# Graph network kernel: five TensorE signals by drains, one GpSimd wait per slot instead of three

## Chip, cores and metric

One core of one Trainium2 chip runs the kernel. The metric is the device time of one execution in microseconds (us), median over the runs. Lower is better. A core has five engines that run their own instruction streams and meet only at semaphores: TensorE (PE, matmuls), VectorE (DVE), ScalarE (ACT), GpSimd (POOL) and SyncE (SP, which issues plain DMAs). Data of the kernel is float32 throughout.

## What is computed

A layer norm with ReLU on 12500 nodes of 128 features, then one graph layer over 200000 edges whose destinations are sorted, and a residual. Cut to what matters:

```python
h = relu(layernorm(x))                                   # 12500 x 128
l1 = linear(h)                                           # per node
w = silu(silu(rbf(dist) @ fc_w1) @ fc_w2) @ fc_w3        # 200000 x 128, per edge
g = l1[edge_src]                                         # gather of 200000 rows
msg = [w00*gs*sh0, w11*dot(gv, sh1), w01*gs*sh1, w10*gv*sh0]   # 200000 x 256
agg = segment_sum(msg, edge_dst) / count
x = x + sc(h) + tanh(agg_s @ alpha_w) * linear2(agg)
```

## The kernel before, in words

**Three stages.** The first stage (some 65 us) normalises the nodes and stores `l1` as `lin_table` in HBM. The second stage, which takes nearly all the time, walks over the edges. The third stage (some 12 us) finishes the last node blocks.

**The walk over the edges.** Edges are cut into 261 groups of 768 (`GROUP`, six tiles of 128). Four groups make a step (`SLOTS` = 4, `u` is the slot, `i` the step), and 65 steps and one short group make up the edges. Every engine has a function `body` with its own fixed order of work for slots `u` = 0 to 3; nothing but semaphores ties the engines together. Counters are compared with `n = i * SLOTS + u`, the group's number.

**GpSimd** (`gather`, L954) only gathers: for each group it issues six indirect DMAs of 128 rows from `lin_table` into the slot's six tiles of `lin_g` (L970, 1563 in all). There are four slots, so group n overwrites what group n-4 used. Before tile 0 it waits until `near_ready` shows group n-4 (L958), before tile 2 until `h2_done` reaches n (L964), before tile 4 until `sums_ready` shows group n-4 (L967). All three are counted up by TensorE. Each wait stands on a `nop`.

**TensorE** in iteration u does, in this order: `layer1` of group n+3 (L999, 4 matmul records), `layer2` of n+2 (L1008), `layer3` of n+1 (L1018, writes `ps_w`), `segment_sum` of n-1 (L1040, writes `ps_sums`), `near_layer` of n (L1030, 12 records, writes `ps_near`). The last matmul of each step carries the signal: `h1_done`, `h2_done`, `w_ready`, `sums_ready`, `near_ready`. `segment_sum` waits for ScalarE's copy of `ps_near` and for VectorE's `agg_ready`; `near_layer` waits for `msg_ready` of its group.

**ScalarE** in iteration u: `silu1` (L1139, after `h1_done`), `silu2` (L1145, after `h2_done`), `copy_w` of n+1 (L1167, after `w_ready`; the trace calls its output `key_all`), `scale_lin` of n+2 (L1157, six tiles, after the gather of n+2), `copy_near` of n (L1172, after `near_ready`).

**VectorE** in iteration u: `accumulate` of n-2 (L1474, two additions into `agg`, after `sums_ready`, with a register load from SBUF at L1469 ahead), `products` of n+2 (L1383 waits for the gather of n+2), `columns`, then `late` of n+1 (L1415 waits for `copy_w`; its last instruction L1423 signals `msg_ready`), and once in four groups the radial basis (L1333 to L1367). `late` of group n is the last reader of that group's slot of `lin_g`.

Of the kernel before, what the change touches and what calls it, by code (L numbers as in the profile page):

```python
# [37 lines left out]
P = 128  # L38
# [8 lines left out]
SLOTS = 4  # L47
# [4 lines left out]
SEG = QUAD // SEGS  # L52
UNIT = 2 * SEG
# [7 lines left out]
NEAR = P // HALVES  # L61
# [10 lines left out]
MSG = 8 * MUL  # L72
# [50 lines left out]
def gnn_kernel(nc, x, src, dst, sh, dist, node_vec, sc_ws, sc_wv, lin1_ws, lin1_wv,  # L123
# [44 lines left out]
    with ExitStack() as top:  # L168
        def sb(name, shape, dt=F32, ctx=top):
            return ctx.enter_context(nc.sbuf_tensor(name, shape, dt))  # L170
# [4 lines left out]
        w1 = sb("w1", [P, SEGS // 2, P])  # L175
        w2 = sb("w2", [P, P])
        w3 = sb("w3", [P, 2, P])
# [26 lines left out]
        with ExitStack() as st:  # L204
# [3 lines left out]
            def sem(name):  # L208
                return st.enter_context(nc.semaphore(name))
# [424 lines left out]
        with ExitStack() as st:  # L634
            def s2(name, shape, dt=F32):
                return sb(name, shape, dt, st)
# [21 lines left out]
            near_sums = s2("near_sums", [P, 2, MSG + 1])  # L658
            far_hot = s2("far_hot", [P, SLOTS, P])
# [7 lines left out]
            rbf = s2("rbf", [P, SEG])  # L667
            h1 = s2("h1", [P, 2, UNIT])
            h2 = s2("h2", [P, 2, UNIT])
            onehot = s2("onehot", [P, SLOTS, TILES, NEAR])  # L670
# [4 lines left out]
            msg = s2("msg", [P, 2, TILES, MSG + 1])  # L675
# [10 lines left out]
            ps_h1 = st.enter_context(nc.psum_tensor("ps_h1", [P, 512], F32))  # L686
            ps_h2 = st.enter_context(nc.psum_tensor("ps_h2", [P, 512], F32))
            ps_w = st.enter_context(nc.psum_tensor("ps_w", [P, 8 * P], F32))
            ps_near = st.enter_context(nc.psum_tensor("ps_near", [P, 512], F32))
# [9 lines left out]
            def sums_bank(i):  # L699

                return ps_h1 if last_group(i) else ps_sums

            def ps_nodes(i):
                return sums_bank(i)[:, 0:COLS]
# [19 lines left out]
            h1_done, h1_ready, h2_done, h2_ready = sem("h1_done"), sem("h1_ready"), sem("h2_done"), sem("h2_ready")  # L724
            w_ready, w_copied, w_read = sem("w_ready"), sem("w_copied"), sem("w_read")
            msg_ready, sums_ready = sem("msg_ready"), sem("sums_ready")
# [4 lines left out]
            near_ready, near_copied = sem("near_ready"), sem("near_copied")  # L731
# [9 lines left out]
            def held(i):  # L741

                return slice(0, TILES, HALVES) if isinstance(i, int) and i == ITERS else slice(0, TILES)
# [19 lines left out]
            def src_loads(s):  # L763

                return 16 * (s.full + (1 if s.phase else 0))
# [54 lines left out]
            with nc.Fori(0, passes):  # L820
                nc.sync.sem_clear(range(sems[0].num, sems[0].num + len(sems)))
                nc.all_engine_barrier()
                with nc.Block() as block:
# [128 lines left out]
                    @block.gpsimd  # L952
                    def _(pool):
                        def gather(s, u, first=False):  # L954
                            if not first:
                                if u == 0:
                                    pool.wait_ge(src_in[s.phase], src_loads(s))
                                pool.wait_ge(near_ready, s.i * SLOTS + u - SLOTS + 1)  # L958
                                pool.nop(nofuse=True)
                            rows = slice(0, LAST_ROWS if isinstance(s.i, int) and s.i == ITERS else P)  # L960
                            tiles = range(TILES)[held(s.i)]
                            for k, t in enumerate(tiles):
                                if not first and k == 2:
                                    pool.wait_ge(h2_done, s.i * SLOTS + u)  # L964
                                    pool.nop(nofuse=True)
                                if not first and k == 4:
                                    pool.wait_ge(sums_ready, s.i * SLOTS + u - SLOTS + 1)  # L967
                                    pool.nop(nofuse=True)
                                col = t % HALVES * PAIRS + t // HALVES
                                pool.indirect_dma_start(  # L970
                                    slot_tiles(s, u)[rows, t, :], None, lin_table,
                                    bass.IndirectOffsetOnAxis(ap=src_ix[rows, s.phase, u, col:col + 1], axis=0)).then_inc(gathered[u], 16)

                        for b in range(OB):
                            pool.wait_ge(lin_stored[b], 16 * (len(range(b, STEPS, OB)) + (REST if b == STEPS % OB else 0)))
                        for u in range(SLOTS):
                            gather(turn_of(0), u, first=True)
                        with pool.Fori(0, (ITERS - 2) // RING) as t:
                            for k in range(RING):
                                for u in range(SLOTS):  # L980
                                    gather(turn_in(t, 1, k), u)
                        for u in range(SLOTS):
                            gather(turn_of(ITERS - 1), u)
                        gather(turn_of(ITERS), 0)

                        for u in range(SLOTS):
                            pool.wait_ge(gathered[u], landed(turn_of(ITERS if u == 0 else ITERS - 1), u))
                        pool.dma_reset()

                    @block.tensor  # L990
                    def _(pe):
                        def layer1(i, k):
                            i, k = i + k // UNITS, k % UNITS
                            if k == 0:
                                pe.wait_ge(rbf_ready, i + 1)
                            at_least(pe, h1_ready, i * UNITS + k)
                            rows = slice(k * 4 * RBF, (k + 1) * 4 * RBF)
                            for part in range(2):
                                mm = pe.matmul(ps_h1[:, part * SEG:(part + 1) * SEG], w1[rows, 2 * k + part, :], rbf[rows, :],  # L999
                                               start=True, stop=True)  # L1000
                            mm.then_inc(h1_done, 1)

                        def layer2(i, k, first=False):
                            i, k = i + k // UNITS, k % UNITS
                            if first:
                                pe.wait_ge(h1_ready, k + 1)
                            at_least(pe, h2_ready, i * UNITS + k)
                            pe.matmul(ps_h2[:, 0:UNIT], w2[:], h1[:, k % 2, :], start=True, stop=True).then_inc(h2_done, 1)  # L1008

                        def layer3(i, u):  # L1010

                            i, u = i + u // SLOTS, u % SLOTS
                            if isinstance(i, int) and (i == ITERS or (i == 0 and u == 0)):
                                pe.wait_ge(h2_ready, i * UNITS + u + 1)
                            at_least(pe, w_copied, i * SLOTS + u)
                            cols = h2[:, u % 2, :].rearrange("p (c j) -> p j c", j=PAIRS)
                            for j in range(PAIRS):
                                mm = pe.matmul(ps_w[:, 2 * j * P:(2 * j + 2) * P], cols[:, j, :], w3[:], start=True, stop=True)  # L1018
                            mm.then_inc(w_ready, 1)

                        def near_layer(i, u):

                            n = i * SLOTS + u
                            pe.wait_ge(msg_ready, n + 1)
                            if isinstance(i, int) and i == ITERS:
                                pe.wait_ge(near_copied, n)
                            for j in range(PAIRS):
                                for half in range(1 if isinstance(i, int) and i == ITERS else HALVES):
                                    t = j * HALVES + half
                                    mm = pe.matmul(ps_near[half * NEAR:(half + 1) * NEAR, 0:MSG + 1], onehot[:, u, t, :], msg[:, u % 2, t, :],  # L1030
                                                   start=(j == 0), stop=(j == PAIRS - 1))
                            mm.then_inc(near_ready, 1)

                        def segment_sum(i, u):

                            n = i * SLOTS + u
                            pe.wait_ge(near_copied, n + 1)
                            if not last_group(i):
                                pe.wait_ge(agg_ready, n + 1)
                            pe.matmul(ps_nodes(i), far_hot[:, u, :], near_sums[:, u % 2, :], start=True, stop=True).then_inc(sums_ready, 1)  # L1040

                        def turn_early(n, k):

# [641 lines left out]
```

## Time and profile before

| | |
|---|---|
| median of 3 runs | 2211.73 us (2203.23 to 2214.47) |
| span of the profiled execution | 2483.8 us |
| of it, stage with the gathers | 68 to 2455 us |
| mean granted TensorE clock | 0.826 |
| DMA, mean | 63 GB/s |

The profiled execution took 272 us more than the median of the runs. The page gives per engine the busy time and its share of the span. Views of the trace give, for a line of the kernel, how often it ran, how long one took, and how long its engine stood idle ahead of it and what ended that idle time. "issue" there means that the profile shows nothing that was waited for, "remote" that a semaphore came whose sender the profile could not tell.

### The profile page before, as it was taken

The page shows a single profiled execution, that of the slowest core. Times are in us where ns is not written, and L with a number is a line of the kernel's source. Part 1 is how long each engine was busy: PE and PEld are TensorE (multiplying, and loading weights), DVE is VectorE, ACT ScalarE, POOL GpSimd, SP SyncE. Part 2 cuts the span into 40 slices and gives each one's busy share as a digit, 9 for nine tenths or more (in the row PEclk, how much of TensorE's full clock was granted, in tenths as well). Part 3 has the DMA queues.
Part 4 walks back from the last instruction along what each step waited for, and adds up shares of the span by engine and source line. Part 5 has one row for each costly group of instructions (what it writes and reads, how often), then busy time and mean ns, then how long its engine had stood idle before and what let it go on. Part 6 is the DMA issues. An engine that isn't in the chain of part 4 may idle for free. (4 is left out here: it accounts for less than half of the span.)

```text
span 2483.8 us, 34021 instructions
## 1 busy us (share of the span) xinstructions
PE 1811.4 (73%) x7969; PEld 1174.2 (47%) x7969; DVE 1783.0 (72%) x4669; ACT 1199.1 (48%) x3310; POOL 1578.4 (64%) x1624
## 2 busy tenths in 40 slices
PE   6577777787777777767677767667787776877777
PEld 6344444454444444444444434444554444544544
DVE  8577767767776777767676667767677776777777
ACT  6354545455454555444444344445444444445443
POOL 7566666666666666666666666666666666666563
PEclk9588878878888887788787878888888888888889
DMA  7322222222222222222122222222222222222222
GB/s 214 70 64 67 56 64 66 66 56 66 66 59 62 67 65 56 55 48 50 46 50 48 48 48 49 54 50 64 57 67 62 59 65 66 53 64 61 59 66 55
DMA packets 347699, 155.73 MB, mean 63 GB/s; under 512 B 237983, under 2 KB 322048, under 8 KB 347584
## 3 DMA queue, kind: packets, MB, share of 16 engines
q0 software_dynamic: 50016, 102.51, 15.7%
q1 hardware_dynamic: 296938, 51.75, 11.4%
q14 instruction: 86, 0.70, 0.1%
q8 instruction: 29, 0.48, 0.1%
q10 hardware_dynamic: 630, 0.29, 0.0%
HBM read 134.27 MB, written 20.15 MB: 62 GB/s over the span
## 5 line engine op out<-in xcount | busy, mean ns | idle before, releaser
L970 POOL DMA_INDIRECT lin_g<-lin_table,src_ix x1563 | 1530.0, 979 | 865.1 <-issue 441.5
L1157 ACT ACTIVATE lin_sh<-lin_g,harm 128x128 f32<-128x128 f32 x1563 | 483.8, 396 | 94.6 <-DMA lin_g<-lin_table,src_ix 87.6
L1040 PE MATMUL ps_sums<-near_sums,far_hot 128*128 128x257 f32 x520 | 208.0, 488 | 440.8 <-DVE agg L1474 206.0
L1030 PE MATMUL ps_near<-msg,onehot 128*64 128x257 f32 x3126 | 507.5, 471 | 1.2 <-DVE msg L1423 1.2
L1018 PE MATMUL ps_w<-w,h 128*128 128x256 f32 x1566 | 462.6, 440 | 28.2 <-ACT key_all L1167 18.5
L1018 PEld LDWEIGHTS ps_w<-w,h 128*128 128x128 f32 x1566 | 395.3, 272 | 135.4 <-issue 44.9
L999 PE MATMUL ps_h<-rbf,w 32*128 32x192 f32 x1044 | 277.0, 390 | 138.0 <-issue 67.1
L1415 DVE TENSOR_TENSOR msg<-lin_sh,key_all 128x576 f32<-128x576 f32 (+1 forms) x261 | 197.3, 756 | 249.9 <-ACT key_all L1167 209.5
L1167 ACT ACTIVATE key_all<-ps_w 128x768 f32<-128x768 f32 x261 | 213.5, 818 | 305.2 <-remote 188.6
L1030 PEld LDWEIGHTS ps_near<-msg,onehot 128*64 128x64 f32 x3126 | 241.3, 164 | 230.6 <-issue 175.7
L1383 DVE TENSOR_TENSOR lin_sh<-lin_g,ps_meta 128x576 f32<-128x576 f32 (+1 forms) x261 | 196.6, 753 | 212.2 <-DMA lin_g<-lin_table,src_ix 207.0
L1040 PEld LDWEIGHTS ps_sums<-near_sums,far_hot 128*128 128x128 f32 x520 | 105.1, 230 | 503.9 <-issue 387.7
L1172 ACT ACTIVATE near_sums<-ps_near 128x257 f32<-128x257 f32 x261 | 99.4, 381 | 474.1 <-remote 342.1
L999 PEld LDWEIGHTS ps_h<-rbf,w 32*128 32x128 f32 x1044 | 189.1, 212 | 228.0 <-issue 176.2
L1008 PE MATMUL ps_h<-h,w 128*128 128x384 f32 x522 | 278.8, 620 | 0.4 <-issue 0.3
L1474 DVE SCALAR_TENSOR_TENSOR agg<-ps_sums,at_lo,agg 128x257 f32 x260 | 126.1, 485 | 190.7 <-issue 188.0
L1401 DVE TENSOR_REDUCE dot<-lin_sh 128x192 f32<-128x576 f32 (+1 forms) x261 | 210.5, 806 | 0.0
L1139 ACT ACTIVATE h<-ps_h 128x384 f32<-128x384 f32 x261 | 127.8, 490 | 141.2 <-remote 74.0
L1423 DVE TENSOR_TENSOR msg<-w_s,ps_meta 128x576 f32<-128x576 f32 (+1 forms) x261 | 195.2, 748 | 0.0
L1145 ACT ACTIVATE h<-ps_h 128x384 f32<-128x384 f32 x261 | 129.1, 494 | 82.9 <-PE ps_h L1008 40.4
L1398 DVE TENSOR_TENSOR onehot<-iota,ps_meta 128x384 f32<-128x384 f32 (+1 forms) x261 | 142.8, 547 | 0.0
L1474 DVE SCALAR_TENSOR_TENSOR agg<-ps_sums,at_hi,agg 128x257 f32 x260 | 123.8, 476 | 0.0
(175 smaller groups left out, 1655.2 us busy)
## 6 DMA issues: line engine op xcount, KB each, us to landing
lin_g<-lin_table,src_ix POOLq DMA_INDIRECT x1563
dist_in<-in_edge_weight SPq DMA_DIRECT2D x67, 96.0 KB
lin_table<-lin_out SPq DMA_DIRECT2D x24, 256.0 KB, 2.6
x_in<-in_x SPq DMA_DIRECT2D x24, 256.0 KB
skip_table<-x_in SPq DMA_DIRECT2D x24, 256.0 KB
xq<-in_x SPq DMA_DIRECT2D x23, 256.0 KB, 3.9
harm<-in_edge_attr SPq DMA_DIRECT2D x66, 48.0 KB
x_in<-skip_table SPq DMA_DIRECT2D x8, 256.0 KB
```

Of the source, the lines that this page charges most:

```text
L970: pool.indirect_dma_start(slot_tiles(s, u)[rows, t, :], None, lin_table, bass.IndirectOffsetOnAxis(ap=src_ix[rows, s.phase, u, col:col + 1 ...
L999: mm = pe.matmul(ps_h1[:, part * SEG:(part + 1) * SEG], w1[rows, 2 * k + part, :], rbf[rows, :], start=True, stop=True)
L1008: pe.matmul(ps_h2[:, 0:UNIT], w2[:], h1[:, k % 2, :], start=True, stop=True).then_inc(h2_done, 1)
L1018: mm = pe.matmul(ps_w[:, 2 * j * P:(2 * j + 2) * P], cols[:, j, :], w3[:], start=True, stop=True)
L1030: mm = pe.matmul(ps_near[half * NEAR:(half + 1) * NEAR, 0:MSG + 1], onehot[:, u, t, :], msg[:, u % 2, t, :], start=(j == 0), stop=(j == PA ...
L1040: pe.matmul(ps_nodes(i), far_hot[:, u, :], near_sums[:, u % 2, :], start=True, stop=True).then_inc(sums_ready, 1)
L1157: last = act.activation(lin_sh0[:, u % 2, j, :], slot_tiles(s, u)[:, j, :], ACT.Copy, scale=harm[:, s.phase, u, harm_col(j):harm_col(j) + 1])
L1167: act.activation(w_sb[:, u % 2, :], ps_w[:, 0:TILES * P], ACT.Copy).then_inc(w_copied, 1)
L1383: dve.tensor_tensor(lin_sh[:, h], lin_v(s, u)[:, h], sh_vec(u)[:, h], ALU.mult).then_inc(lin_sh_ready, 1)
L1401: dve.tensor_reduce(dot[:, u % 2, h], lin_sh[:, h].rearrange("p t m c -> p t c m"), AX_X, ALU.add).then_inc(dot_ready, 1)
L1415: dve.tensor_tensor(o10[:, h], scaled[:, h, MUL:].rearrange("p t (m c) -> p t m c", m=3), spread_m(w_part(u, 2))[:, h], ALU.mult)
L1474: dve.scalar_tensor_tensor(out=rows, in0=ps_nodes(i), scalar=part[:, bass.ds(g, 1)], in1=rows, op0=ALU.mult, op1=ALU.add).then_inc(added, 1)
```

## The change

The diff does two things. Each of the five TensorE steps ends with a separate `drain` instruction, which waits for the matmuls ahead of it and then gives the signal that the last matmul gave before. GpSimd's three waits per group are replaced by one ahead of tile 0: for `msg_ready` of group n-4, VectorE's last instruction on that group. The wait on `src_in` for slot 0 stays.

```diff
-                                pool.wait_ge(near_ready, s.i * SLOTS + u - SLOTS + 1)
+                                pool.wait_ge(msg_ready, s.i * SLOTS + u - SLOTS + 1)
                                 pool.nop(nofuse=True)
...
-                            for k, t in enumerate(tiles):
-                                if not first and k == 2:
-                                    pool.wait_ge(h2_done, s.i * SLOTS + u)
-                                    pool.nop(nofuse=True)
-                                if not first and k == 4:
-                                    pool.wait_ge(sums_ready, s.i * SLOTS + u - SLOTS + 1)
-                                    pool.nop(nofuse=True)
+                            for t in tiles:
...
-                            mm.then_inc(h1_done, 1)
+                            pe.drain(fusable=False).then_inc(h1_done, 1)
...
-                            pe.matmul(ps_h2[:, 0:UNIT], w2[:], h1[:, k % 2, :], start=True, stop=True).then_inc(h2_done, 1)
+                            pe.matmul(ps_h2[:, 0:UNIT], w2[:], h1[:, k % 2, :], start=True, stop=True)
+                            pe.drain(fusable=False).then_inc(h2_done, 1)
...
-                            mm.then_inc(w_ready, 1)
+                            pe.drain(fusable=False).then_inc(w_ready, 1)
...
-                            mm.then_inc(near_ready, 1)
+                            pe.drain(fusable=False).then_inc(near_ready, 1)
...
-                            pe.matmul(ps_nodes(i), far_hot[:, u, :], near_sums[:, u % 2, :], start=True, stop=True).then_inc(sums_ready, 1)
+                            pe.matmul(ps_nodes(i), far_hot[:, u, :], near_sums[:, u % 2, :], start=True, stop=True)
+                            pe.drain(fusable=False).then_inc(sums_ready, 1)
```

## Rows read from the trace of the kernel before

**Rows 1.** The page: busy us, share of the span, instructions per engine.

```profile
PE 1811.4 (73%) x7969; PEld 1174.2 (47%) x7969; DVE 1783.0 (72%) x4669; ACT 1199.1 (48%) x3310; POOL 1578.4 (64%) x1624
```

**Rows 2.** Gather line: busy us, mean ns, idle ahead; then min/median/max ns.

```profile
L970 POOL DMA_INDIRECT lin_g<-lin_table,src_ix x1563 | 1530.0, 979 | 865.1 <-issue 441.5
...
L970 POOL DMA_INDIRECT lin_g<-lin_table,src_ix x1563: 917/944/1694, 68.1 to 2454.4; - x196
```

**Rows 3.** Timeline of GpSimd: start us, us, instruction, idle ahead; first, typical, last gather.

```profile
68.09 1.12 POOL L970 DMA_INDIRECT lin_g<-lin_table,src_ix  x1 [7.92 <-issue]
...
1010.28 0.94 POOL L970 DMA_INDIRECT lin_g<-lin_table,src_ix  x1 [0.30 <-issue]
...
2454.36 0.92 POOL L970 DMA_INDIRECT lin_g<-lin_table,src_ix  x1 [1.82 <-PE ps_h L1008]
```

**Rows 4.** Waits of GpSimd: us in total, times, longest us.

```profile
POOL lin_g L970 <- remote: 325.1, 155, 3.2
POOL lin_g L970 <- PE ps_sums L1040: 41.7, 27, 4.7
POOL lin_g L970 <- PE ps_h L1008: 40.9, 21, 9.3
POOL lin_g L970 <- PE ps_near L1030: 15.9, 13, 6.9
```

**Rows 5.** Waits of VectorE and ScalarE, same columns.

```profile
DVE msg L1415 <- ACT key_all L1167: 209.5, 113, 4.4
DVE lin_sh L1383 <- DMA lin_g<-lin_table,src_ix: 207.0, 137, 4.0
DVE agg L1474 <- issue: 188.0, 215, 7.3
...
ACT lin_sh L1157 <- DMA lin_g<-lin_table,src_ix: 87.6, 51, 4.5
```

**Rows 6.** Timeline of TensorE, one group at the full clock: start, us.

```profile
1026.67 0.70 PE L1040 MATMUL ps_sums<-near_sums,far_hot 128*128 128x257 f32 x2 [2.35 <-ACT near_sums L1172]
1027.30 1.52 PE L1030 MATMUL ps_near<-msg,onehot 128*64 128x257 f32 x12
1028.75 0.91 PE L999 MATMUL ps_h<-rbf,w 32*128 32x192 f32 x4
1029.60 0.91 PE L1008 MATMUL ps_h<-h,w 128*128 128x384 f32 x2
1030.35 1.46 PE L1018 MATMUL ps_w<-w,h 128*128 128x256 f32 x6
```

**Rows 7.** The same five steps in a half-clock stretch.

```profile
1001.95 1.20 PE L1040 MATMUL ps_sums<-near_sums,far_hot 128*128 128x257 f32 x2 [4.29 <-issue]
1003.08 2.84 PE L1030 MATMUL ps_near<-msg,onehot 128*64 128x257 f32 x12
1005.85 1.65 PE L999 MATMUL ps_h<-rbf,w 32*128 32x192 f32 x4
1007.42 1.65 PE L1008 MATMUL ps_h<-h,w 128*128 128x384 f32 x2
1008.87 2.77 PE L1018 MATMUL ps_w<-w,h 128*128 128x256 f32 x6
```

**Rows 8.** Stretches: length, busy by engine, granted clock (PEclk), DMA share, GB/s.

```profile
1002.00:1010.00 8.00, 8.00 (x23) 4.60 (x24) 6.54 (x13) 3.33 (x11) 4.75 (x5) 0.50 0.32 53
...
97.00:2455.00 2358.00, 1734.39 (x7510) 1113.16 (x7510) 1696.91 (x4267) 1136.54 (x3132) 1507.56 (x1541) 0.82 0.26 58
```

**Rows 9.** Timeline of TensorE and ScalarE from 1017 us, around two signals.

```profile
1017.20 1.46 PE L1018 MATMUL ps_w<-w,h 128*128 128x256 f32 x6
1018.49 0.60 PE L1040 MATMUL ps_sums<-near_sums,far_hot 128*128 128x257 f32 x2
1019.02 1.52 PE L1030 MATMUL ps_near<-msg,onehot 128*64 128x257 f32 x12
...
1021.83 0.81 ACT L1167 ACTIVATE key_all<-ps_w 128x768 f32<-128x768 f32 x1 [3.94 <-remote]
...
1026.23 0.39 ACT L1172 ACTIVATE near_sums<-ps_near 128x257 f32<-128x257 f32 x1 [1.85 <-remote]
```

**Rows 10.** A TensorE drain at a stage's end, ns and start; the last matmuls ahead.

```profile
L823 PEldq DRAIN  x1: 750/750/750, 2470.5 to 2470.5; - x1
...
2470.46 0.70 PE L1040 MATMUL ps_h<-near_sums,far_hot 128*128 128x257 f32 x2 [0.48 <-ACT near_sums L1172]
```

More of the change, by code:

```diff
@@ L998, in layer1 @@
                             for part in range(2):
-                                mm = pe.matmul(ps_h1[:, part * SEG:(part + 1) * SEG], w1[rows, 2 * k + part, :], rbf[rows, :],
+                                pe.matmul(ps_h1[:, part * SEG:(part + 1) * SEG], w1[rows, 2 * k + part, :], rbf[rows, :],
                                                start=True, stop=True)
-                            mm.then_inc(h1_done, 1)
+                            pe.drain(fusable=False).then_inc(h1_done, 1)
                         def layer2(i, k, first=False):
@@ L1017, in layer3 @@
                             for j in range(PAIRS):
-                                mm = pe.matmul(ps_w[:, 2 * j * P:(2 * j + 2) * P], cols[:, j, :], w3[:], start=True, stop=True)
-                            mm.then_inc(w_ready, 1)
+                                pe.matmul(ps_w[:, 2 * j * P:(2 * j + 2) * P], cols[:, j, :], w3[:], start=True, stop=True)
+                            pe.drain(fusable=False).then_inc(w_ready, 1)
                         def near_layer(i, u):
@@ L1029, in near_layer @@
                                     t = j * HALVES + half
-                                    mm = pe.matmul(ps_near[half * NEAR:(half + 1) * NEAR, 0:MSG + 1], onehot[:, u, t, :], msg[:, u % 2, t, :],
+                                    pe.matmul(ps_near[half * NEAR:(half + 1) * NEAR, 0:MSG + 1], onehot[:, u, t, :], msg[:, u % 2, t, :],
                                                    start=(j == 0), stop=(j == PAIRS - 1))
-                            mm.then_inc(near_ready, 1)
+                            pe.drain(fusable=False).then_inc(near_ready, 1)
                         def segment_sum(i, u):
```

## The prediction, made before the result was known

> **What bounds the kernel now.** I read the page's busy line first [rows 1]. No engine is full: TensorE 73%, VectorE 72%, GpSimd 64%. But busy time leaves out what an engine spends between instructions, so the second view is the gather line itself [rows 2, 3]. A gather takes 0.979 us on GpSimd and even with nothing to wait for the next one starts 0.30 us later. So 1563 of them need 1530.0 + 1562 x 0.30 = 1999 us. The first starts at 68.1, and 28.5 us follow the end of the last (2455.3 to 2483.8). That makes a floor of 68.1 + 1999 + 28.5 = 2096 us, if GpSimd never waits. The profiled span of 2483.8 lies 388 us above it, and the waits of GpSimd explain this: they add up to 423.6 us, the usual 0.30 us before each gather included [rows 4].
>
> The third view is who waits for the gathers. VectorE waited 207.0 us for them in 137 of 261 groups, ScalarE 87.6 us in 51 [rows 5]. So in over half the groups the gather is what comes last, and it comes late because GpSimd was held by TensorE's signals. VectorE's other large waits are 209.5 us (113 times) for ScalarE's copy of `ps_w`, which hangs on TensorE, and 188.0 us "issue" ahead of L1474, where it loads a register. The fourth view is TensorE's steps. At the full clock a group takes 0.70 + 1.52 + 0.91 + 0.91 + 1.46 = 5.5 us [rows 6]; in a stretch with granted clock 0.50, that is the 1.2 GHz level, it takes 1.20 + 2.84 + 1.65 + 1.65 + 2.77 = 10.1 us [rows 7, 8]. GpSimd needs 1999 / 261 = 7.66 us for a group. Thus three engines are near the bound together: GpSimd by its count, VectorE by its busy time and register load (1783.0 + 188.0 = 1971 us), TensorE wherever its clock is at the lower level.
>
> **The profiled execution against the runs.** It took 2483.8 us, the median of the runs is 2211.7. The runs lie only 2211.7 - 2096 = 116 us above the gather floor, if gathers cost the same there. One thing that the profiled execution shows, and that may be smaller without the profiler, is late signals [rows 9]: `ps_w` was done at 1018.66 and ScalarE, idle, started on it at 1021.83; `ps_near` was done at 1020.54 and ScalarE started at 1026.23, again after idle time. Both waits are put down as "remote", as are 325.1 us of GpSimd's [rows 4]. I make the sum in the profiled execution and then carry over the share of the distance to the floor that stays, 388 us there and 116 us in the runs.
>
> The Trainium skill, Perfetto Trace Analysis, section Tensor Engine Instruction, says that a matmul's end in a profile is an estimate and that its semaphore goes out when PSUM has acknowledged the writes. The trace agrees [rows 9] that signal and shown end can part, here by 3.2 us and 5.7 us; no run shown here says whether a drain's signal would be earlier.
>
> **GpSimd's waits, removed and moved.** Three waits and three `nop`s per group become one of each. The removed `nop`s are worth nothing: gathers with and without one ahead show the same 0.30 us. The waits matter. In VectorE's order `late` of group n-4 runs in iteration n-5; `near_layer` of n-4 follows on TensorE in iteration n-4, and its `segment_sum` in iteration n-3. VectorE needs the gather of n in iteration n-2. So today the last two gathers of a group (2 x 1.28 = 2.6 us and the landing) are released only one iteration ahead of use; after the change all six are released about two iterations ahead, some 15 us, for 7.66 us of gathering. A TensorE delay of a few microseconds then no longer reaches GpSimd. Queued behind the new wait are only GpSimd's own gathers; SyncE's loads are untouched, and it waits for `msg_ready` and `quot_ready` as before.
>
> What it is worth: VectorE's 207.0 us go, at most all, at least nothing if the same time is then spent waiting for `ps_w`. I take all 207.0, since nothing else on GpSimd is left to hold a gather but its own pace, 7.66 us a group against 9.0 us (2358 / 261) in the profiled execution [rows 8]. ScalarE's 87.6 us lie in `scale_lin`, ahead of `copy_near`, which TensorE's L1040 waits for; much of it is the same late gathers, so I take half, 44 us, with ends 0 and 88.
>
> **Five drains per group on TensorE.** A drain holds the next step until the last matmul is through. Today the next step's first matmul starts before the shown end of the last: by 0.07, 0.07, 0.06 and 0.16 us [rows 6], and by 0.17 us from L1018 to L1040 [rows 9], together 0.53 us a group. The only drains of TensorE in the trace end each within 0.1 us of the matmul before them: one runs from 2470.5 to 2471.25, the matmuls end at 2471.16 [rows 10]. I take 0.05 us each. So 0.53 + 0.25 = 0.8 us a group. The bounds: below nothing it goes only by earlier signals, up to the 207.0 + 44 us already counted again; above, the next step's weights can no longer be loaded ahead and each step starts anew, up to about 0.5 us a drain, as the weight load and first matmul of a released step stand together before the second (L1040 takes 0.70 us when released, 0.60 us when not [rows 6, 9], so 0.1 us of it is seen).
>
> At the full clock 5.5 + 0.8 = 6.3 us stays under the 7.66 us of GpSimd: that work hides it. Where VectorE waits for `ps_w`, nothing does: from `accumulate` through L1040, L1030, L999, L1008 and L1018 to `ps_w` the loop passes all five drains. That is 113 waits x 0.8 = 90 us.
>
> The Trainium skill, TensorE: Matmul & The Clock Gate, sections Step-by-step and Single matmul latency, speaks against this part: matmuls overlap the emptying of one with the filling of the next, and a single one pays a constant of about 166 ns at the full clock on top of its columns. By that, as an estimate of the page, five drains would cost 0.83 us a group; the trace shows 0.53 us of overlap to lose [rows 6, 9], so the sum would be nearly the same.
>
> **The sum.** Profiled: 2483.8 - 207.0 - 44 + 90 = 2323 us. Above the floor of 2096 that is 227 of 388 us, 0.585. In the runs: 2096 + 0.585 x 116 = **2164 us**, 2.2% under 2211.7.
>
> **The rivals.** *The waits were the worst of it* (chance 0.14). If the late signals also rule the undisturbed runs, or if TensorE, released earlier, keeps its clock up, the kernel comes to GpSimd's pace: 2096 plus some 10 us, 2106. For it: the 7.66 us pace is only 5% under the runs' 8.1 us a group (2358 - 272 = 2086, over 261, is 8.0). Against: VectorE needs 1971 us by itself and has almost no room to catch up.
>
> *The gather is not what counts* (0.14). GpSimd's waits only fill time that VectorE then waits for `ps_w` instead; or the new wait holds GpSimd as long. Then 2212, give or take 10. For it: 113 waits for `ps_w` stand beside the 137 for gathers. Against: those for gathers stand first in VectorE's order, and ScalarE has them too.
>
> *The drains put TensorE on the path* (0.24), slower. In the lower-clock stretches TensorE's 10.1 us a group are already over GpSimd's 7.66. The mean clock of 0.82 [rows 8] puts 36% of 2358 us there, some 84 groups, and there each microsecond of drains is one of time. At x us a drain the kernel gives 2164 + 84 x (5x - 0.8). It passes 2212 at x = 0.27 us. At 0.35 us it is 2164 + 84 x 0.95 = 2244; at 0.5 us 2307, and then at the full clock 5.5 + 2.5 = 8.0 us would be over 7.66 too. For it: half-clock steps overlap more, L1018's start at 1008.87 lies 0.20 us before L1008's end [rows 7], and the profile cannot show what a restart behind a drain costs. Against: both drains that I see end promptly.
>
> **How the numbers follow.** The forecast holds 0.48. A change under 0.5%, 11 us, cannot be told from none. Faster by more: 0.48 + 0.14 = 0.62. Same: 0.14. Slower: 0.24. The range runs from 2096, less a few us in case gathers cost a little less without the profiler, to the slower rival at 0.37 us a drain: 2092 to 2255. Beyond it I leave the dear drains and a gather pace well under that of the trace. The likeliest case alone, with its terms between their ends, is 2120 to 2195.
>
> **What would show it.** In the changed kernel's profile GpSimd's waits for TensorE should be gone and its whole idle time be near 1563 x 0.30 us. VectorE's wait for gathers should fall under 50 us, its wait for ScalarE's `key_all` should be the largest. Drains would appear on TensorE's queue, and the start of L1030 should lie some 0.15 us later against L1040's end. If L999 to L1018 take over 1.5 us more a group, the slower rival holds. If the profiled span falls by hundreds of microseconds but the runs' median hardly, the late signals belonged to the profiler. If gathers still come last in half the groups, GpSimd's own pace is the bound and the time is near 2106.

## The result, and the profile after

The changed kernel takes 2247.5 us (2231.91 to 2252.18), 1.015 times the kernel before (95% interval 1.012 to 1.019). It was forecast at 2164 us, 2.2% faster; it is 1.5% slower, and the rival that said so was given 0.24. A later measurement of the same kernel, beside other runs of the kernel before, gave 1.0206 (1.0173 to 1.0240): 2243.03 against 2200.77 us.

The page's first lines of the changed kernel:

```profile
span 2230.1 us, 34624 instructions
...
PE 1774.5 (80%) x7969; PEld 1061.7 (48%) x7969; DVE 1780.7 (80%) x4669; ACT 1243.2 (56%) x3310; POOL 1577.9 (71%) x1624
```

Its waits (us in total, times, longest), the lines that answer to [rows 4, 5]:

```profile
POOL lin_g L964 <- issue: 458.6, 1473, 7.7
...
DVE msg L1411 <- ACT key_all L1163: 194.2, 111, 5.4
DVE agg L1470 <- issue: 188.6, 215, 7.9
...
PE ps_sums L1035 <- DVE agg L1470: 139.1, 73, 8.9
POOL lin_g L964 <- DVE msg L1419: 138.9, 89, 8.3
```

VectorE no longer waits for gathers at all: it has no such line any more, where it had 207.0 us [rows 5]. GpSimd waits for nothing but VectorE's message, 138.9 us. What is left is VectorE's wait for ScalarE's copy of `ps_w`, 194.2 us. By the profiles alone the change looks like a gain of 10%: a span of 2483.8 us before and 2230.1 us after. The timed runs say the opposite, and that contradiction is where the prediction went wrong.

Each drain has a row of its own on TensorE's queue (x count, ns min/median/max); its time is mostly that of the matmuls it waits for. The first is behind `layer2`, the second behind `layer3`:

```profile
L1003 PEldq DRAIN  x261: 815/888/1625, 81.5 to 2199.1; - x131
...
L1014 PEldq DRAIN  x261: 1448/1603/2927, 86.8 to 2204.4; - x131
```

And TensorE's steps at the full clock, one group (start us, us), the lines that answer to [rows 6]:

```profile
1007.30 0.67 PE L1035 MATMUL ps_sums<-near_sums,far_hot 128*128 128x257 f32 x2 [0.23 <-issue]
1008.06 1.52 PE L1025 MATMUL ps_near<-msg,onehot 128*64 128x257 f32 x12
1009.80 0.91 PE L993 MATMUL ps_h<-rbf,w 32*128 32x192 f32 x4 [0.22 <-issue]
1010.79 0.91 PE L1002 MATMUL ps_h<-h,w 128*128 128x384 f32 x2
1011.78 1.62 PE L1013 MATMUL ps_w<-w,h 128*128 128x256 f32 x6
1013.63 0.67 PE L1035 MATMUL ps_sums<-near_sums,far_hot 128*128 128x257 f32 x2 [0.23 <-issue]
```

From `segment_sum` to the next one it is 1013.63 - 1007.30 = 6.33 us. This group is typical: the medians of the five steps over the stretches at the full clock add up to 6.32 us, and to 4.86 us in the second profile of before, below. Every step now starts 0.08 to 0.23 us after the end of the last, where it used to start 0.06 to 0.17 us before it.

### The profile page after: what moved, and what is told of

Read it like the earlier page. It is cut to its first block and busy times, and to the rows that moved or that the text cites. A ratio compares the mean times of both kernels' runs of the same rounds, so it can differ in the third digit from the quotient of the medians.

```text
span 2230.1 us, 34624 instructions
## 1 busy us (share of the span) xinstructions
PE 1774.5 (80%) x7969; PEld 1061.7 (48%) x7969; DVE 1780.7 (80%) x4669; ACT 1243.2 (56%) x3310; POOL 1577.9 (71%) x1624
## 5 line engine op out<-in xcount | busy, mean ns | idle before, releaser
L964 POOL DMA_INDIRECT lin_g<-lin_table,src_ix x1563 | 1528.9, 978 | 597.9 <-issue 458.6
L1013 PE MATMUL ps_w<-w,h 128*128 128x256 f32 x1566 | 486.0, 454 | 27.0 <-issue 9.2
L1013 PEld LDWEIGHTS ps_w<-w,h 128*128 128x128 f32 x1566 | 364.4, 267 | 216.2 <-issue 198.2
L1025 PE MATMUL ps_near<-msg,onehot 128*64 128x257 f32 x3126 | 424.6, 408 | 28.3 <-issue 9.2
L1411 DVE TENSOR_TENSOR msg<-lin_sh,key_all 128x576 f32<-128x576 f32 (+1 forms) x261 | 197.0, 755 | 206.6 <-ACT key_all L1163 194.2
L993 PE MATMUL ps_h<-rbf,w 32*128 32x192 f32 x1044 | 244.2, 354 | 142.7 <-DVE rbf L1363 104.0
L1035 PE MATMUL ps_sums<-near_sums,far_hot 128*128 128x257 f32 x520 | 192.0, 453 | 184.7 <-DVE agg L1470 139.1
L1025 PEld LDWEIGHTS ps_near<-msg,onehot 128*64 128x64 f32 x3126 | 217.6, 143 | 222.6 <-issue 155.1
L1002 PE MATMUL ps_h<-h,w 128*128 128x384 f32 x522 | 252.9, 568 | 27.1 <-issue 9.7
L993 PEld LDWEIGHTS ps_h<-rbf,w 32*128 32x128 f32 x1044 | 165.9, 189 | 223.5 <-issue 177.3
L1035 PEld LDWEIGHTS ps_sums<-near_sums,far_hot 128*128 128x128 f32 x520 | 85.6, 207 | 282.0 <-issue 282.0
L1002 PEld LDWEIGHTS ps_h<-h,w 128*128 128x128 f32 x522 | 80.9, 195 | 104.7 <-issue 104.7
```

The lines of the kernel that those rows point to most:

```text
L964: pool.indirect_dma_start(slot_tiles(s, u)[rows, t, :], None, lin_table, bass.IndirectOffsetOnAxis(ap=src_ix[rows, s.phase, u, col:col + 1 ...
L1411: dve.tensor_tensor(o10[:, h], scaled[:, h, MUL:].rearrange("p t (m c) -> p t m c", m=3), spread_m(w_part(u, 2))[:, h], ALU.mult)
```

## The experiments

All ratios are against the kernel before, measured on the same chip as the kernel in question, with the 95% interval. The microseconds put on a difference of ratios are that difference times 2202 us, the median of the kernel before in these runs (2201 to 2204).

**The kernel before, profiled a second time.** No edit.

> The kernel before once more, unchanged, for a second profiled execution. Theory A (the profiled execution that the prediction was built on was not like the timed ones): span near 2200 us, no waits put down as remote, VectorE's wait for gathers under 100 us where the first showed 207.0. Theory B (profiling this kernel always delays TensorE's signals, and drains cure that): span near 2480 us again, with hundreds of us of remote waits.

Its span was 2199.1 us, its waits:

```profile
PE ps_sums L1040 <- DVE agg L1474: 354.3, 100, 11.2
...
ACT lin_sh L1157 <- DMA lin_g<-lin_table,src_ix: 189.1, 101, 4.6
...
DVE lin_sh L1383 <- DMA lin_g<-lin_table,src_ix: 116.6, 119, 2.4
...
POOL lin_g L970 <- PE ps_sums L1040: 82.5, 87, 7.2
DVE msg L1415 <- ACT key_all L1167: 55.8, 78, 4.3
POOL lin_g L970 <- PE ps_h L1008: 55.7, 82, 7.1
...
POOL lin_g L970 <- PE ps_near L1030: 18.3, 60, 0.3
```

No wait is put down as remote. Theory A holds on span and on the remote waits; on the gathers it asked for under 100 us, and there are 116.6, ScalarE's even 189.1. So the gathers did come late in the ordinary execution too, but VectorE's wait for `ps_w` was 55.8 us and not 209.5 [rows 5]. The first profiled execution was one in which TensorE's signals came late [rows 9]. Neither profiling as such nor the lack of drains causes that, as this execution was profiled in the same way and has no drains. What did cause it in that one execution stays open. Its trace is also incomplete: it holds 14926 records of semaphore updates, where this one holds 40591 and each of the other twelve 40510 to 40676. So that trace does not tell for every wait what ended it. Its late signals are real all the same: each of its 373 remote waits was ended by a recorded signal at least 1.5 us behind the shown end of the last step that sends it, 4.7 us in the median. For `ps_w` in [rows 9] the signal is at 1021.80 us, 3.1 us behind the shown end.

**GpSimd's part alone**: one wait for the message, no drains.

```diff
-                                pool.wait_ge(near_ready, s.i * SLOTS + u - SLOTS + 1)
+                                pool.wait_ge(msg_ready, s.i * SLOTS + u - SLOTS + 1)
...
-                                if not first and k == 2:
-                                    pool.wait_ge(h2_done, s.i * SLOTS + u)
-                                    pool.nop(nofuse=True)
-                                if not first and k == 4:
-                                    pool.wait_ge(sums_ready, s.i * SLOTS + u - SLOTS + 1)
-                                    pool.nop(nofuse=True)
```

> The kernel before with GpSimd's part of the change alone: one wait for VectorE's message, no drains. Theory A (the drains cost more than the gather part gives): faster than before, 2160 to 2200 us, and over 40 us under the changed kernel's 2247. Theory B (the gathers running ahead do the harm, drains are cheap): 2235 to 2260 us. Theory C (the gather part is worth nothing outside the profiled execution of before): 2205 to 2220 us. In its profile GpSimd's waits for TensorE are gone in all of them.

2143.87 us, ratio 0.9738 (0.9712 to 0.9764): 2.6% faster than the kernel before, and faster than the changed kernel by over 4% of the before. Its waits:

```profile
PE ps_sums L1034 <- DVE agg L1468: 316.7, 121, 10.7
...
DVE msg L1409 <- ACT key_all L1161: 105.7, 90, 3.9
...
POOL lin_g L964 <- DVE msg L1417: 62.9, 74, 7.1
...
DVE lin_sh L1377 <- DMA lin_g<-lin_table,src_ix: 7.8, 12, 2.4
```

Against the second profile of before, VectorE's wait for gathers fell by 116.6 - 7.8 = 109 us, its wait for `ps_w` rose by 105.7 - 55.8 = 50 us. The net is 59 us, and the spans differ by 2199.1 - 2140.2 = 58.9 us. Nearly half of what the gathers gave went into the next wait. Theory A holds in kind, and its range of 2160 to 2200 us was too cautious; B and C are out. This is the fastest kernel of this study.

**The drains alone**, with GpSimd's three waits kept.

```diff
-                            mm.then_inc(h1_done, 1)
+                            pe.drain(fusable=False).then_inc(h1_done, 1)
```

and the same for `h2_done`, `w_ready`, `near_ready` and `sums_ready`.

> The kernel before with the five drains alone; GpSimd keeps its three waits per group. Theory A: slower than the changed kernel or as slow, 2250 to 2330 us, since TensorE's delays now also hold the gathers. Theory B: as before, 2205 to 2220 us. Theory C: as the changed kernel, 2235 to 2260 us.

2273.6 us, ratio 1.0324 (1.0288 to 1.0361), 71 us for the drains by themselves, as Theory A had it. The two parts of the change do not simply add: GpSimd's part gives 58 us without drains, but only 26 to 38 us where the drains stand (1.0324 against 1.0206 and 1.0152, on two chips). GpSimd's waits for the drains are 125.8 us for the one behind `segment_sum` and 73.6 us for the one behind `layer2`:

```profile
POOL lin_g L970 <- PEq L1042: 125.8, 75, 7.1
...
POOL lin_g L970 <- PEq L1009: 73.6, 73, 8.5
```

**One part of GpSimd's waits**: the kernel before with only `near_ready` ahead of tile 0, the waits ahead of tiles 2 and 4 removed.

> The kernel before, without drains, and GpSimd keeps only its first wait, near_ready of group n-4; the waits ahead of tiles 2 and 4 are gone. If the two later waits did the harm, since they release the last four gathers only one iteration ahead of use: ratio to before near the 0.974 of GpSimd's whole part. If it was that the first wait stands on TensorE and not on VectorE's message: ratio 0.99 to 1.00.

2174.43 us, ratio 0.9867 (0.9850 to 0.9883). That lies between the two answers: the two later waits account for 29 us of the 58, the move of the first from TensorE's signal to VectorE's message for the other half. VectorE's wait for gathers stands in between as well:

```profile
DVE lin_sh L1377 <- DMA lin_g<-lin_table,src_ix: 55.3, 77, 2.4
```

**Drains that signal nothing.** The changed kernel with `then_inc` back on the last matmul, the drain behind it.

```diff
-                            pe.drain(fusable=False).then_inc(w_ready, 1)
+                            mm.then_inc(w_ready, 1)
+                            pe.drain(fusable=False)
```

> The changed kernel, but the last matmul of each step gives the signal and the drain behind it signals nothing. If what costs is that the drain holds back the next step: as the changed kernel, 2240 to 2255 us. If what costs is that a drain's signal goes out later than a matmul's: close to the kernel with GpSimd's part alone. If the late signals in the profile of before come from completions that pile up while TensorE runs on, they are gone here too, and the profiled span is within 1% of the other runs.

2262.96 us, ratio 1.0285 (1.0249 to 1.0321). Holding back the next step costs; the way of the signal does not save anything. It came out even 0.8 to 1.3 points dearer than the changed kernel (1.0152 and 1.0206, on other chips) and above its own range of 2240 to 2255 us. So this test finds no cost in a drain's signal as against a matmul's. Part of the extra is in TensorE's steps: at the full clock their medians add up to 6.42 us a group here and 6.32 in the changed kernel, 26 us over 261 groups. Why they are longer was not pursued.

**Two drains at each step's end.**

```diff
+                            pe.drain(fusable=False)
                             pe.drain(fusable=False).then_inc(w_ready, 1)
```

> The changed kernel with two drains at each step's end instead of one, the second with the signal: ten per group. If a drain costs its own fixed time of about 0.05 us beside the emptying, the second adds 5 x 0.05 x 261 = 65 us of TensorE time, and at most 30 us to the kernel, 2250 to 2280 us. If nearly all of the price is the emptying of the array, which the second finds done: 2240 to 2255 us.

2296.1 us, ratio 1.0428 (1.0400 to 1.0457), 49 to 61 us over the changed kernel. That is more than either forecast. The timeline shows what the second one costs, at the full clock:

```profile
1000.35 0.91 PE L993 MATMUL ps_h<-rbf,w 32*128 32x192 f32 x4 [0.30 <-issue]
1001.42 0.91 PE L1003 MATMUL ps_h<-h,w 128*128 128x384 f32 x2 [0.16 <-issue]
1002.48 1.62 PE L1015 MATMUL ps_w<-w,h 128*128 128x256 f32 x6 [0.16 <-issue]
1004.41 0.67 PE L1039 MATMUL ps_sums<-near_sums,far_hot 128*128 128x257 f32 x2 [0.31 <-issue]
```

The step from L1003 to L1015 takes 1.06 us here, against 0.99 us in the changed kernel. Some groups are slower: the next one in the same trace takes 1.20 us for it. The medians of the five steps add up to 6.75 us a group, 0.43 us more than with one drain each. So a drain behind a drain, with nothing left to empty, still costs 0.07 to 0.11 us, in all 0.43 x 261 = 112 us of TensorE's time if every group ran at the full clock, and about half of it reached the end.

**Which drain.** GpSimd's part and some of the drains: behind layers 1, 2 and 3; behind `segment_sum` and `near_layer`; and one by one behind `layer1`, `layer2`, `layer3`.

> GpSimd's part of the change and three of the five drains: behind layer1, layer2 and layer3, those between agg_ready and ps_w last in TensorE's order. The five cost about 95 us together. If each drain on the loop from accumulate to ps_w counts alike: three fifths, 57 us over the kernel without drains, ratio to before near 1.00. If what counts is VectorE's wait for ps_w alone and the drains nearest to it: 80 to 95 us, ratio 1.01 to 1.02.

> GpSimd's part of the change and the other two drains: behind segment_sum and near_layer. If each drain counts alike: two fifths, 38 us over the kernel without drains, ratio to before near 0.99. If only the drains ahead of ps_w count: under 15 us, ratio 0.975 to 0.98.

> GpSimd's part of the change and one drain, behind layer1. In the changed kernel's trace each drain lengthens the time from its step to the next by its own amount: 0.15 us behind layer1, 0.40 us behind layer2 (0.16 of it as layer3 runs longer), 0.46 us behind layer3. Theory D (TensorE's time counts wherever it is spent): the three share the 97 us that they cost together in that proportion, so 14 us here, ratio to before 0.98. Theory E (only what lies ahead of the signal for ps_w counts, since behind layer3 TensorE often waits for VectorE anyway): 25 us, ratio 0.985.

> GpSimd's part of the change and one drain, behind layer2. Theory D: 38 us over the kernel without drains, ratio 0.991. Theory E: 65 us, ratio 1.003.

> GpSimd's part of the change and one drain, behind layer3, whose emptying falls where TensorE waited 316.7 us for VectorE's accumulate in the kernel without drains. Theory D: 44 us over the kernel without drains, ratio 0.994. Theory E: under 15 us, ratio under 0.981.

| drains behind | added to a TensorE group, full clock | ratio (95%) | over the kernel without drains | VectorE's wait for `ps_w` | granted clock |
|---|---|---|---|---|---|
| none | | 0.9738 (0.9712 to 0.9764) | | 105.7 us | 0.884 |
| layer3 | 0.47 us | 0.9779 (0.9756 to 0.9803) | 9 us | 92.9 us | 0.886 |
| segment_sum, near_layer | 0.44 us | 0.9792 (0.9772 to 0.9812) | 12 us | 119.0 us | 0.902 |
| layer1 | 0.15 us | 0.9815 (0.9786 to 0.9843) | 17 us | 130.3 us | 0.884 |
| layer2 | 0.40 us | 0.9983 (0.9962 to 1.0003) | 54 us | 162.6 us | 0.884 |
| layers 1, 2, 3 | 1.02 us | 1.0219 (1.0177 to 1.0261) | 106 us | 209.1 us | 0.903 |
| all five | 1.46 us | 1.0152 and 1.0206 | 91 and 103 us | 194.2 and 201.7 us | 0.916 and 0.920 |

The second column compares the usual time from the start of one step to the start of the next at the full clock; the last is the mean over the profiled execution.

The differences carry 7 to 9 us either way, so 9, 12 and 17 us are hardly told apart. The drain behind `layer2` stands out. In its trace:

```profile
1000.01 0.91 PE L993 MATMUL ps_h<-rbf,w 32*128 32x192 f32 x4
1000.85 0.91 PE L1002 MATMUL ps_h<-h,w 128*128 128x384 f32 x2
1001.84 1.62 PE L1013 MATMUL ps_w<-w,h 128*128 128x256 f32 x6
1004.44 0.67 PE L1035 MATMUL ps_sums<-near_sums,far_hot 128*128 128x257 f32 x2 [0.97 <-DVE agg L1469]
```

`layer2` to `layer3` is 0.99 us here against 0.75 us in [rows 6], and `layer3` itself takes 1.62 us against 1.46: 0.40 us in all, right ahead of `ps_w`. The longer `layer3` is the weight load that no longer runs ahead. Without drains the load starts 0.33 us before `layer3`'s first matmul, here it starts with it, first without and then with the drain:

```profile
1001.13 1.44 PEld L1012 LDWEIGHTS ps_w<-w,h 128*128 128x128 f32 x6
...
1001.84 1.29 PEld L1013 LDWEIGHTS ps_w<-w,h 128*128 128x128 f32 x6 [0.69 <-issue]
```

The drain behind `layer3` costs TensorE about as much (1.69 us against 1.29 from its start to that of `segment_sum`, and 0.07 us more to `near_layer`). But it gives the signal for `ps_w` itself, and ScalarE's wait for it is no longer than before (256.8 us against 262.5). What it holds back is `segment_sum`, a step that often waits for VectorE anyway: 0.97 us in the last row of the timeline above, 316.7 us in 121 groups over the kernel without drains. Two rows of its profile:

```profile
DVE msg L1409 <- ACT key_all L1161: 92.9, 87, 3.9
...
DVE lin_sh L1377 <- DMA lin_g<-lin_table,src_ix: 30.6, 27, 2.5
```

So place decides, more than size, and that is Theory E in kind. Theory D fails on `layer3`, which it put at 44 us and which measured 9. For `layer2` the measured 54 us lies between D's 38 and E's 65, and for `layer1` 17 us fits D's 14 and E's 25 alike. With the drain behind `layer3` VectorE's wait for `ps_w` did not grow, but its waits for gathers went from 7.8 to 30.6 us. Why, this run does not show.

Being ahead of `ps_w` is not the whole rule either. In TensorE's order the drains behind `segment_sum` and `near_layer` also lie between VectorE's `agg` and `ps_w`, and of their 0.44 x 261 = 115 us only 12 reached the end, under the 15 us of that run's second answer. No run shows what takes up the rest. Drains also do not add up: one by one those behind layers 1, 2 and 3 cost 80 us, together 106, a gap of 26 us, give or take 17, and more than either answer expected of that run (57, and 80 to 95). And each total is net of a clock that changes with it. At two levels, 1.0 and 0.5 of the full clock, a mean of 0.884 is some 500 us at the lower one, 0.902 with the two drains some 425 us, 0.916 with all five some 375 us. What part of the cost this gave back no run here separates.

**The changed kernel again**, beside the single drains.

> The changed kernel once more, beside the kernels with one drain. Its ratio was 1.015, and that of the kernel with only three of its five drains 1.022. If the two drains behind segment_sum and near_layer really give something back where the other three stand: 1.010 to 1.018 again. If the difference was that of two sessions: 1.02 to 1.03.

2243.03 us, ratio 1.0206 (1.0173 to 1.0240), the same as with three drains within the intervals. That is the second answer: the lower 1.0152 of the first time is put down to the difference between two measurements, and nothing shows that the two drains behind `segment_sum` and `near_layer` give anything back.

## Why the prediction was wrong, step by step

**The basis.** The sum was made in an execution of 2483.8 us, 12% over the runs. It noted the gap and the late signals [rows 9], and then carried over "the share of the distance to the floor that stays". That is the step that failed. It multiplies every term by 116 / 388 = 0.3, gain and cost alike. In the runs the forecast therefore held 251 x 0.3 = 75 us of gain from the gathers and 90 x 0.3 = 27 us of cost from the drains, 48 us net. The gain came out near that size, the cost at over three times it.

**The gathers' term.** 75 us were forecast, 58 measured (ratio 0.9738). Right in sign, and the size nearly; the second profile of before shows where the rest went: of VectorE's 109 us, 50 turn into waiting for `ps_w`. The prediction named that as the lower end of this term and booked nothing for it. That 0.3 of terms from a disturbed execution gives 75 us, near the measured 58, is luck: no run bears out the factor.

**The drains' term.** 27 us were forecast for the runs, 91 to 103 measured with GpSimd's part in place and 71 with the old waits. A fixed addition to a loop need not shrink because other waits in it do, and here it did not. Unscaled, the 90 us would have come out right: from the kernel without drains to the changed one VectorE's wait for `ps_w` rises by 194.2 - 105.7 = 88.5 us and the span by 89.9 us. With the forecast's own gain for the gathers this would have given 2212 - 75 + 90 = 2227 us, and with the measured one 2244. But that the 90 us fit is luck too: it is 113 waits at 0.8 us, and the price of a group was nearly twice that.

**The price of a drain.** 0.8 us a group was forecast. At the full clock a group took 1.45 + 0.85 + 0.75 + 1.29 + 0.53 = 4.87 us from start to start before [rows 6, 9] and takes 6.33 us after, so it is 1.46 us. Three things were left out: the step after a drain starts 0.08 to 0.23 us behind the end, not at 0.05, together 0.70 us and not 0.25; `layer3` becomes 0.16 us longer; and `segment_sum` 0.07 us. The row of a drain at the stage's end [rows 10] showed how fast a drain ends, not how long the next step takes to start. At 1.46 x 261 = 381 us of TensorE's time, 91 to 103 us reached the end, about a quarter; the sum had counted its full price of 0.8 us in 113 groups. "The loop passes all five drains" was therefore too simple: two of the five cost 12 us by themselves.

**The slower rival.** With 1.46 / 5 = 0.29 us a drain its own threshold of 0.27 us was passed. Its place was wrong, though: it put the cost in the lower-clock stretches, and those shrank: the granted clock is 0.856 in the second profile of before, 0.884 with GpSimd's part and 0.916 after the change. Most of VectorE's added wait for `ps_w` lies at the full clock: sorted by the clock granted when the wait ended, it went from 88.4 to 158.5 us there and from 17.3 to 35.7 us at the lower one. The sign named for this rival, over 1.5 us more a group from L999 to L1018, would have denied it: the measured addition is 3.60 - 3.06 = 0.54 us, and the kernel is slower all the same.

The Trainium skill, TensorE: Matmul & The Clock Gate, section Single matmul latency, gives the constant of about 166 ns at the full clock for a single matmul that the prediction cited. Its estimate from that, 0.83 us a group, is too low against the measured 1.46 us: 0.15 us each behind `layer1` and `segment_sum` is near the constant, but it is 0.29 us behind `near_layer` and 0.40 and 0.47 us behind `layer2` and `layer3`.

**What was right.** The waits of GpSimd on TensorE went as described; VectorE no longer waits for a gather; `near_layer` starts 0.16 us later against the end of `segment_sum`, as its sign asked; VectorE's largest wait is the one for `key_all`, as forecast; the span fell by hundreds of microseconds while the runs' median did not, which the prediction had named as the sign that the late signals did not belong to the timed runs. It took them for the profiler's; the second profile of before shows that they were that one execution's. One sign was missed: GpSimd's whole idle time was to be near 469 us and is 597.9, as it now waits 138.9 us for VectorE's message.

**The other rivals.** That the waits were the worst of it, at GpSimd's pace, 2106 us: not reached even without drains, at 2143.87 us, as GpSimd then still waits 62.9 us for VectorE. That the gather does not count: out, by 58 us. (The prediction writes the runs' pace as 8.1 us a group in one place; its own sum gives 8.0. Nothing hangs on it.)

## What to carry to other kernels

If a profiled execution is 12% longer than the timed runs, or hundreds of its waits are remote, take another before anything is added up from it; and if that can't be had, do not scale down a cost that the change adds to a loop along with the waits. A drain in place of a signal on the last matmul was no better signal and cost 0.15 to 0.47 us of TensorE's time at the full clock here. Ahead of a step that often waits anyway nearly all of it was hidden (`layer3`, 9 us); one or two steps ahead of the result that another engine waits for, about half was paid (`layer1` and `layer2`). One wait on the last reader of the gathered buffer, in place of three on TensorE, gave 2.6% by itself.

## What was not expected of the hardware

The kernels with drains ran longer and at a higher granted TensorE clock, 0.916 with five a group and 0.921 with ten, against 0.884 without. A higher mean clock was no sign of a faster kernel. Which level is granted when was not studied.

In one profiled execution TensorE's signals arrived several microseconds after the matmuls' shown ends, and nearly two thirds of the semaphore records were missing; in the other one of the same kernel no wait was remote. A second drain behind a first is not free: 0.07 to 0.11 us each.
